# Half of the value product of an attention kernel in split fp32r parts, with the low parts of the probabilities on POOL

## What is computed

```python
def attention(x, w_qkv, w_out):                  # x is the normalised input
    q, k, v = split(einsum('bsd,od->bso', x, w_qkv))      # 16 heads of 128 each
    q, k = rope(q), rope(k)                      # x*cos + rotate_half(x)*sin
    attn = softmax(einsum('bqhd,bkhd->bhqk', q, k) / sqrt(128))
    return einsum('bhqk,bkhd->bqhd', attn, v).reshape(B, S, 16*128) @ w_out.T

def ffn(x):
    h = gelu(x @ dequant(mxfp4(up_kernel)) + up_bias)
    return h @ dequant(mxfp4(down_kernel)) + down_bias

xn = layernorm(x)
out = x + attention(xn, w_qkv, w_out) + ffn(xn)
```

## Time and profile before

| what | value |
|---|---|
| median of 3 runs | 2506.6 us (2505.27 to 2508.3) |
| the profiled execution: its own time | 2508.02 us |
| the profiled execution: its span in the trace | 2506.2 us |
| instructions in the span | 41398 |
| mean granted clock of PE | 0.995 of full speed |

### The profile page before, as it was taken

The page is one execution under the profiler, slowest core; times in us unless marked ns, Lnnn a source line. Parts: engine busy times, 40 slices in busy tenths (PEclk is TensorE's granted clock), DMA queues, the critical chain, the costliest instruction groups (busy, mean ns, idle before and its releaser), DMA issues. The chain is left out here.

```text
span 2506.2 us, 41398 instructions
## 1 busy us (share of the span) xinstructions
PE 2457.5 (98%) x12656; PEld 2139.8 (85%) x12656; DVE 1982.2 (79%) x3204; ACT 1437.6 (57%) x2648; POOL 1392.9 (56%) x1115
## 2 busy tenths in 40 slices
PE   6999999999999999999999999999999999999899
PEld 4888888888888888888888888888888888888688
DVE  6877878787887878788787878878787887878576
ACT  5656666565656566565656556655555566565233
POOL 6567656665655555565556555655555565555031
PEclk9999999999999999999999999999999999999999
DMA  4665666656665555656665655656575565655842
GB/s 135 167 168 151 173 159 161 172 157 189 179 163 147 151 153 153 157 146 188 173 164 143 160 150 151 159 146 185 152 183 146 151 159 152 158 140 144 231 141 68
DMA packets 267289, 396.28 MB, mean 158 GB/s; under 512 B 38496, under 2 KB 120800, under 8 KB 267104
## 3 DMA queue, kind: packets, MB, share of 16 engines
q1 hardware_dynamic: 267232, 395.67, 59.9%
HBM read 91.43 MB, written 35.65 MB: 51 GB/s over the span
## 5 line engine op out<-in xcount | busy, mean ns | idle before, releaser
L1020 PE MATMUL o_ps<-keys_first,v_rows 128*128 128x256 f32 x4096 | 930.9, 381 | 10.4 <-DMA keys_first<-turned_blocks 10.4
L1020 PEld LDWEIGHTS o_ps<-keys_first,v_rows 128*128 128x128 f32 x4096 | 767.7, 191 | 110.4 <-DMA keys_first<-turned_blocks 11.6
L1020 PE MATMUL s_ps<-seq_parts 128*128 128x512 f32 x3072 | 834.3, 409 | 12.7 <-ACT probs L689 8.0
L792 DVE TENSOR_REDUCE neg_max<-s_ps 128x1 f32<-128x1024 f32 x512 | 611.3, 1203 | 160.3 <-PE s_ps L1020 160.1
L689 ACT ACTIVATE probs<-s_ps,neg_max 128x1024 f32<-128x1024 f32 x512 | 568.7, 1111 | 247.9 <-DVE neg_max L792 241.7
L1020 PEld LDWEIGHTS s_ps<-seq_parts 128*128 128x128 f32 x3072 | 577.9, 189 | 133.6 <-ACT probs L689 12.1
L804 DVE STREAM_TRANSPOSE turned_blocks<-probs 128x512 f32<-128x512 f32 x1024 | 662.9, 685 | 32.2 <-ACT probs L689 10.3
L558 POOL TENSOR_TENSOR rope_a<-rope_a,cos 128x512 f32<-128x512 f32 x250 | 324.6, 1298 | 633.1 <-ACT rope_b L673 633.1
L563 POOL TENSOR_TENSOR seq_parts<-rope_a,seq_parts 128x512 fp32r<-128x512 f32 x250 | 320.5, 1282 | 288.4 <-ACT seq_parts L680 288.4
L1020 PE MATMUL slot_ps<-seq_parts,w_parts 128*128 128x512 f32 x1506 | 386.9, 392 | 4.8 <-DMA seq_parts<-xnt_parts 4.8
L680 ACT ACTIVATE seq_parts<-rope_a 128x512 fp32r<-128x512 f32 x250 | 157.6, 630 | 387.9 <-POOL rope_a L561 386.4
(11 more groups left out here) (111 smaller groups left out, 1733.6 us busy)
## 6 DMA issues: line engine op xcount, KB each, us to landing
keys_first<-turned_blocks SPq DMA_DIRECT2D x2048, 128.0 KB, 2.7
w_parts<-w_qkv_parts SPq DMA_DIRECT2D x72, 512.0 KB, 4.3
seq_parts<-xnt_parts SPq DMA_DIRECT2D x14, 1024.0 KB, 8.3
w_qkv_parts<-w_parts SPq DMA_DIRECT2D x24, 512.0 KB, 3.7
wo_parts<-w_out_parts SPq DMA_DIRECT2D x48, 256.0 KB, 3.1
w_raw<-in_w_qkv SPq DMA_DIRECT2D x24, 256.0 KB, 4.3
y<-in_x SPq DMA_DIRECT2D x16, 256.0 KB, 3.3
ln_x<-in_x SPq DMA_DIRECT2D x16, 256.0 KB, 3.4
```

The costliest lines, as they stand in the source:

```text
L792: nc.vector.tensor_reduce(neg_max[:, k2 % 16:k2 % 16 + 1], s_ps[k2 % 2][:, :], AXX, ALU.max, negate=True).then_inc(max_ready, 1)
L1020: ins = nc.tensor.matmul(out, w, m, start=(n == 0), stop=(n == len(terms) - 1))
```

## The change

**The value product.** Of the eight key tiles, four (`SPLIT`) are now multiplied in parts: v_hi by p_hi and v_lo by p_hi (L1265, L1266), then v_hi by p_lo (L1277), twelve fp32r matmuls a chunk. The other four stay unsplit (L1258, eight passes). PE does first two unsplit tiles, then the eight products with p_hi, two more unsplit tiles, and last the four with p_lo.

**The parts.** ACT copies the probabilities of the four tiles after the move into p_hi (`probs_high`, 1,024 columns a chunk, at the end of its step). POOL subtracts p_hi from them in place (`probs_low`, two instructions of 512 elements a chunk, FRONT and BACK; the tuple for DVE is empty). Two of the four v groups go to v_hi, and DVE makes v_lo (`v_low`). p_hi and v_lo lie in the fourth block of `seq_parts`.

**The order of the keys.** The keys are ordered by their remainder by four (`by_remainder`), so that one transpose for each query tile does instead of two; q stays as it was, and for k rows ACT's `rotated_high` and POOL's `rotated_low` read with a step of four elements. The moves go by query tile: `move_tile` with four transfers for each, tile 0 of the next chunk at the end of SP's step, tile 1 at the start of the next.

**What moves.** `turn` of tile 0 moves to the end of DVE's step before. POOL's `rotate_rest` is cut into `rotated_sum` and `rotated_low`, which stand at steps written out for each k8; `rotated_high` moves on ACT to match. `GROUPS` gets another order (the first group now in step 2), `MX_PARTS` has thirteen smaller parts in ten steps where there were eight in seven, and LayerNorm's mean and normalisation go from DVE to ACT.

```diff
+SPLIT = 4
...
+        v_rows = sb("v_rows", [P, 2, BT - SPLIT, 2 * HEAD])
+        v_hi = sb("v_hi", [P, 2, SPLIT, 2 * HEAD], F32R)
+        p_hi = seq_parts[:, 3, 0].rearrange("p c s -> p (c s)")[:, 0:2 * SPLIT * CHUNK].rearrange(
+        v_lo = seq_parts[:, 3, 1].rearrange("p c s -> p (c s)")[:, 0:4 * SPLIT * HEAD].rearrange(
...
+        turned_blocks = sb("turned_blocks", [P, 2, 2, QUADS, BT, QUAD])
+        keys_first = sb("keys_first", [P, 2, 2 * QUADS, BT, QUAD], F32R)
...
+        GROUPS = {(2, 1): (0, "qk0", 0), (3, 1): (1, "qk0", 1), (4, 0): (2, "qk0", 2), (4, 1): (3, "v", 0),
+                  (5, 0): (4, "qk0", 3), (6, 0): (5, "v", 1), (6, 1): (6, "qk1", 0), (7, 0): (7, "v", 2),
+                  (7, 1): (8, "qk1", 1), (0, 0): (9, "qk1", 2), (0, 1): (10, "qk1", 3), (1, 0): (11, "v", 3)}
...
+        V_TILES = (1, 2, 0, 3)
+        V_SPLIT = tuple(n for n in range(4) if V_TILES[n] < SPLIT // 2)
+        FRONT, BACK = slice(0, 2), slice(2, SPLIT)
+        BACK_BY_DVE, BACK_BY_POOL = (), (0, 1, 2, 3, 4, 5, 6, 7)
...
+        MX_PARTS = {0: (2,), 2: (3,), 3: (4,), 6: (5,), 7: (6, 7), 8: (8, 9), 10: (10,), 11: (11,), 12: (12,), 15: (0, 1)}
...
+                if t == 0 and c >= 2:
                     sp.wait_ge(o_ready, c - 1)
                 for a in range(QUADS):
-                    for half in range(2):
+                    sp.dma_start(keys_first[:, slot, t * QUADS + a].rearrange("p j q -> p (j q)").bitcast(F32),
+                                 turned_blocks[a * QUAD:(a + 1) * QUAD, slot, t].rearrange("p b j q -> p b (j q)")
+                                 ).then_inc(keys_moved[k % 4], 16)
...
-                    move_chunk(b * SEQ_CHUNKS + n, n, first)
+                    move_tile(b * SEQ_CHUNKS + n, n, 1)
...
+                    if not (last and n == SEQ_CHUNKS - 1):
+                        move_tile(b * SEQ_CHUNKS + n + 1, n + 1, 0)
...
+        def by_remainder(a):
+            return a.rearrange("p (j k b) -> p j b k", k=QUAD, b=QUADS)
...
-            engine.tensor_tensor(hi, a, b, ALU.add).then_inc(own, 1)
+            engine.tensor_tensor(hi, a_in, b_in, ALU.add).then_inc(own, 1)
...
-            return engine.tensor_tensor(lo, a, hi.bitcast(F32), ALU.subtract)
+            return engine.tensor_tensor(lo, total, hi.bitcast(F32), ALU.subtract)
...
+            def rotated_low(p, part, n):
...
+                pool.wait_ge(rope_hi, p * 8 + m - FIRST_ROTATED + 1)
+                total, hi, lo = rope_a[:, m % 2, :], qk_hi[:, head, kind, cols], qk_lo[:, head, kind, cols]
+                if kind == 1:
+                    total, hi, lo = by_remainder(total), as_remainders(hi), as_remainders(lo)
+                nc.gpsimd.tensor_tensor(lo, total, hi.bitcast(F32), ALU.subtract).then_inc(qk_ready, 1)
+            def probs_low(c, k):
+                slot = k % 2
+                pool.wait_ge(p_hi_ready, c + 1)
+                low = keys_first[:, slot, :, FRONT, :]
+                nc.gpsimd.tensor_tensor(low, low.bitcast(F32), p_hi[:, slot, :, FRONT, :].bitcast(F32),
+                                        ALU.subtract).then_inc(p_lo_front, 1)
+                if k % 8 in BACK_BY_POOL:
+                    low = keys_first[:, slot, :, BACK, :]
+                    nc.gpsimd.tensor_tensor(low, low.bitcast(F32), p_hi[:, slot, :, BACK, :].bitcast(F32),
+                                            ALU.subtract).then_inc(p_lo_back_pool, 1)
...
+                if k8 == 0:
+                    if not first:
+                        rotated_low(p, "qk1", 0)
+                        probs_low(c - 1, k - 1)
+                        rotated_sum(p, "qk1", 1)
+                    rotated_sum(p, "qk1", 2)
+                if k8 == 1:
+                    if not first:
+                        rotated_low(p, "qk1", 1)
+                    probs_low(c - 1, k - 1)
+                    rotated_low(p, "qk1", 2)
+                    rotated_sum(p, "qk1", 3)
+                if k8 == 2:
+                    rotated_low(p, "qk1", 3)
+                    probs_low(c - 1, k - 1)
+                if k8 == 3:
+                    probs_low(c - 1, k - 1)
+                    if more_pairs:
+                        rotated_sum(p + 1, "qk0", 0)
+                if k8 == 4:
+                    if more_pairs:
+                        rotated_low(p + 1, "qk0", 0)
+                    probs_low(c - 1, k - 1)
+                    if more_pairs:
+                        rotated_sum(p + 1, "qk0", 1)
+                if k8 == 5:
+                    if more_pairs:
+                        rotated_low(p + 1, "qk0", 1)
+                    probs_low(c - 1, k - 1)
+                    if more_pairs:
+                        rotated_sum(p + 1, "qk0", 2)
+                if k8 == 6:
+                    if more_pairs:
+                        rotated_low(p + 1, "qk0", 2)
+                        rotated_sum(p + 1, "qk0", 3)
+                    probs_low(c - 1, k - 1)
+                    if more_pairs:
+                        rotated_low(p + 1, "qk0", 3)
+                if k8 == 7:
+                    probs_low(c - 1, k - 1)
+                    if more_pairs:
+                        rotated_sum(p + 1, "qk1", 0)
...
+                    total, hi = by_remainder(total), as_remainders(hi)
+                nc.scalar.activation(hi, total, ACT.Copy).then_inc(rope_hi, 1)
...
+            def probs_high(i, k):
+                act.wait_ge(keys_moved[k % 4], chunk_moves(i, k))
+                nc.scalar.activation(p_hi[:, k % 2], keys_first[:, k % 2, :, 0:SPLIT, :].bitcast(F32),
+                                     ACT.Copy).then_inc(p_hi_ready, 1)
...
+            def mean(n, loaded):
+            def normalise(n):
...
+                    if k % 8 == 1:
+                        rotated_high(p, "qk1", 2)
+                    if k % 8 == 2:
+                        rotated_high(p, "qk1", 3)
...
+                    if k % 8 == 6 and more_pairs:
+                        rotated_high(p + 1, "qk0", 3)
+                    if k % 8 == 3 and more_pairs:
+                        rotated_high(p + 1, "qk0", 0)
+                    if k % 8 == 4 and more_pairs:
+                        rotated_high(p + 1, "qk0", 1)
+                    if k % 8 == 5 and more_pairs:
+                        rotated_high(p + 1, "qk0", 2)
+                    if k % 8 == 7 and more_pairs:
+                        rotated_high(p + 1, "qk1", 0)
+                    if k % 8 == 0 and not first:
+                        rotated_high(p, "qk1", 1)
+                    probs_high(i, k)
...
-                for half in range(2):
-                    keys = probs[:, (2 * k + n) % 4, :].rearrange("p (j h q b) -> p h j b q", h=2, q=QUAD, b=2)[:, half]
-                    last = nc.vector.transpose(turned_blocks[:, k % 2, 2 * half:2 * half + 2, :, n, :].rearrange("p b j q -> p j b q"), keys)
-                last.then_inc(blocks_turned, 1)
+                nc.vector.transpose(turned_blocks[:, k % 2, n].rearrange("p b j q -> p j b q"),
+                                    probs[:, (2 * k + n) % 4, :].rearrange("p (j b q) -> p j b q", b=QUADS, q=QUAD)
+                                    ).then_inc(blocks_turned, 1)
...
+            def v_low(p, parity, n, bank):
+                at = 2 * V_TILES[n]
+                dve.wait_ge(v_ready, p * 4 + n + 1)
+                nc.vector.tensor_tensor(v_lo[:, parity, at:at + 2, :], bank.rearrange("p (a b) -> p a b", a=2),
+                                        v_hi[:, parity, at:at + 2, :].bitcast(F32), ALU.subtract).then_inc(v_lo_ready, 1)
...
-                    turn(i, k, 0, first)
+                    turn(i, k, 1, first)
...
-                if not tail:
-                    turn(i, k, 1, first)
+                g = None if tail or (first and k == 0) else group_at(k - 1, 1, last)
+                if g and g[1] == "v" and g[2] in V_SPLIT:
+                    v_low(i * 2 + g[3], g[3] % 2, g[2], slot_ps[:, 1])
...
+                if not tail and not (last and k == 15):
+                    turn(i, k + 1, 0, first)
...
-                      [(v_rows[:, parity, kt, cols], keys_first[:, slot, :, kt, :]) for kt in range(BT)], o_ready)
+                out = o_ps[:, 0:CHUNK]
+                def unsplit(kt, start):
+                    nc.tensor.matmul(out, v_rows[:, parity, kt - SPLIT, cols], keys_first[:, slot, :, kt, :].bitcast(F32),
+                                     start=start, stop=False)
+                for kt in range(SPLIT, BT - 2):
+                    unsplit(kt, kt == SPLIT)
+                pe.wait_ge(p_hi_ready, c + 1)
+                for kt in range(SPLIT):
+                    nc.tensor.matmul(out, v_hi[:, parity, kt, cols], p_hi[:, slot, :, kt, :], start=False, stop=False)
+                    nc.tensor.matmul(out, v_lo[:, parity, kt, cols], p_hi[:, slot, :, kt, :], start=False, stop=False)
+                if k % 8 == 0:
+                    pe.wait_ge(v_ready, p * 4 + 4)
```

(58 more changed lines are left out.)

151 lines of the change are left out of this document (90 added, 61 removed).

## The result

The changed kernel takes 2585.1 us in the median of four runs (2579.7 to 2592.8), the kernel before 2506.4 beside them: a ratio of 1.0316 with a 95% interval from 1.0288 to 1.0343. It is 79 us slower, where 10 us less were forecast.

What follows compares the result with a forecast made beforehand. The prediction took PE (98% busy) to bound the kernel: 2508.0 us less 74 for the value product, plus 34 for step 2 and 29 for the first seven pairs, gives 2497, as median 2496 us; range 2458 to 2555.

Steps and rivals of the forecast that it cites:

- PE's gain: Value product on PE: 3.17 us a chunk instead of 3.46, 74 us less in all, 69.9 us a pair.
- POOL's operations: 512 new probs_low subtractions at 1.25 us each; POOL's busy time goes from 1393 to about 2045 us.
- Rival 2: POOL's operations take longer, 1.49 us for probs_low, and the change is slower: 2512 to 2570 us, chance 0.25.
- Step 2: PE waits for probs_low in step 2 of a pair, 1.35 us on average over 25 pairs: 34 us.
- the 1.0 us of the first pair: PE's forecast wait for probs_low in step 2 of a round's first pair, with probs_low done at 8.73 us.
- First seven pairs: While POOL also makes the next weights' low parts, a pair takes it 73.8 us; 4.2 us lost each, 29 us.
- 2.4 twice and 2.1 once: POOL's waits in the first seven pairs for ACT's rotated_high, probs_high and w_high, where w_low stands between, in us.
- The lock: Two-input DVE instructions and POOL's SBUF reads lock each other out; comparisons take their median, total 2501 us.
- The wait of 2.1 us in a second pair: Step 2's wait in a round's second pair by the lock rule, 2.1 us in place of 1.7.
- Rivals 3 and 4: Late key moves: 2541 us, chance 0.07; fp32r matmuls at 0.15 us instead of 0.12: 2562 us, chance 0.06.

Runs made afterwards that it cites:

- e7_straight: Changed kernel, but ACT's rotated_high and POOL's rotated_low read the k rows straight instead of with a step of four elements: 2565.1 us.
- e4_no_low: Changed kernel with POOL's two probs_low subtractions cut to 8 elements each instead of 512, waits and matmuls kept: 2469.4 us.
- e2_weights_late: Changed kernel with POOL's w_low and wo_low placed behind probs_low in their steps of the first sequence: 2564.8 us.
- e6_both_back_dve: Changed kernel with probs_low first in step 2, weights' low parts behind probs_low, and DVE making every chunk's second subtraction: 2569.4 us.
- f2_before_more: Kernel before the change with two more unsplit matmuls of 16 columns behind each value product, 20 records a chunk: 2628.5 us.

## Why the prediction was wrong

- **PE's gain (74 us)** was right: 3.19 us a chunk, and 70.0 a pair where nothing stalls.
- **POOL's operations** were priced right: probs_low has a median of 1292 and 1291 ns and starts 1.22 to 1.25 apart. (Their sum is 1393 + 640 = 2033 us, not about 2045; POOL measured 2072.) Rival 2 came out on the right side, but its 1.49 us is not there. Its sentence from the Trainium skill (GPSIMD Engine Reference, 7. Performance pitfalls for Q7 kernels) had half as much again; the rows of k show 1.56 against 1.29, a fifth, and e7_straight prices that together with ACT's slower copy at 20 us.
- **Step 2 (34 us)**: the place and the chain were right, and so was the second pair of a round (1.7 us forecast, 1.8 measured). The step that failed is the 1.0 us of the first pair: PE waits 1.75. The prediction gave the quantiser to the second pair alone, but `MX_PARTS` puts the parts of its scale into steps 15 and 0, ahead of the first pair's step 2; that this is the cause is read from the trace, and no run moves it. Each wait also costs more than PE's idle time. In the last 24 pairs step 2 lasted 2.3 and 1.7 us longer than in e4_no_low, 49 us where this term had 32.
- **First seven pairs (29 us)**: the step that failed is "2.4 twice and 2.1 once". The third wait was right (2.06), but POOL's waits for ACT before the weights' other low parts are 2.8 to 4.7 us (4.41 in the row above). A pair took 78.6 us instead of 74.1, 31 us more; 8 of them the kernel before had as well (73.4 a pair where the prediction's sum has 72.2), so 23 are the change's. e2_weights_late takes 20 us back by order alone. The term's own sum isn't clear: 3.9 and a step 2's wait of 1.35 make 5.2 a pair, and it takes 4.2.
- **Costed at nothing, or not at all**: PE's own program grew by four matmul records a chunk, which cost 14 waits of 1.4 us (19.6 us). The lower clock, up to 27 us more, was in no term; up to 12 of them lie in the first seven pairs (seven stretches, 24 us).
- Together: of the 90 us between forecast and result, 23 lie in the first seven pairs, 63 in the next 24 and 4 at the ends. The 63, against the shortest length of each step in e4_no_low: 16 in step 2, 26 where PE's instructions are fetched, 7 where LayerNorm's rows come late (three rounds), 14 in steps 0, 6, 7 and 11, where the scores wait for rotated_low or the output for `o_lo`. What the lower clock costs is contained in these.
- By experiments: order 52 us (2585 to 2533), amount 64 (2533 to 2469), and 37 that stay above 2506 - 74 = 2432, of which the fetch is 18. The prediction looked for both in two places only.
- **The lock**: by that rule of the Trainium skill (SBUF — State Buffer, Who interferes with whom) DVE's comparisons should have grown with POOL's load. Their median fell from 1396 to 1058 ns while POOL went from 56% to 80%; but the change also put them into other steps, so this is no test. e4_no_low is one, as DVE's program is the same: with POOL at 61% their mean falls from 929 to 683 ns and L1042 from 1186 to 383, and both read two inputs in SBUF. That agrees with the rule. Instructions with a single input get shorter as well (L1060, from 1277 to 251 ns), which the prediction had not counted at all. The wait of 2.1 us in a second pair, which the prediction worked out by it, did not come (1.8). The spread of DVE's subtraction in e6_both_back_dve (662 to 1819 ns, about one POOL operation) would fit the rule too.
- **Rivals 3 and 4** fell: PE's waits in the changed kernel name no move of the probabilities, and fp32r matmuls take 0.12. ACT does wait 88.7 us for these moves ahead of its copy; in e4_no_low, with the same moves, a pair still takes 70.0.

## What to carry to other kernels

When work is handed to an engine in order, list what stands in front of it and what each of those instructions waits for: the engine's busy share (80% here) does not show the idle time ahead of the one that matters. Count the instructions of a loop's body on the critical engine before adding to it. Try half of a change whose gain is sure and whose costs sit in the last margin of another engine.

## What was unexpected of the hardware

With 12656 and with 13168 matmul records in the program, q8 shows 18 and 19 packets, so PE's loop of one round was not fetched anew. With 13680 there are 127 more, about nine of 16.4 KB (149 KB) for each of the 14 waits of PE behind the loop's jump, 1.4 us each. e4_no_low confirms the nine: 109 more for 12 waits. The Trainium skill (Runtime: NRT & Kernel Launch, Instruction fetch mechanics) says that PE holds 128 KiB of instructions in blocks of 16 KiB, and that a taken branch to a page outside the current window of two must wait for it. The size of the packets agrees with the first, and the trace shows that such a wait is not hidden here; but the smaller loops, shorter by 4 to 7% of the records, jump back without a wait, which a window of only two pages would not allow. In f2_before_more the waits are 0.9 us each, so the cost of a wait is not fixed.
